# Attention and expert kernel: hand-written orders re-placed, one cast-load earlier, and the flag branches set ahead of the last stores

## The reference

```python
# layernorm of x as the graph's weights ("adj"), two layers of 8-head attention over ctx, elu after each
e = leaky_relu(attn_self[:, :, None] + attn_neigh[:, None, :], 0.2) + MASK_VAL * (1.0 - adj)[None, :, :]
out = elu(einsum('hnm,hmo->hno', softmax(e), feat) + b)
...
x = x + tanh(g_xattn[0]) * xattn(ctx_512, layernorm(x), W0, ..., b1)        # x: 4 x 256 x 256
# experts on xt = layernorm(x): 8 experts of 128 hidden columns, the best 2 of each token weighted
logits = tanh(xt @ Wg1.T) @ Wg2.T
h = silu(einsum('td,ehd->teh', xt, Wup) + bup)
down = einsum('teh,eoh->teo', h, Wdown) + bdown
x = x + tanh(g_ffn[0]) * einsum('te,teo->to', scores, down)
```

## Time and profile before

| | |
|---|---|
| runs | 87.66, 87.21, 87.19 us; median 87.21 |
| the profiled execution | 86.43 us, of which its span (first to last instruction) is 84.6 |
| granted TensorE clock | 0.997 |
| busy, share of the span | PE 90%, PE weight load 85%, DVE 79%, ACT 62%, POOL 47% |
| chain that ended last | PE 75%, DMA 6%, DVE 4%, issue 4%, ACT 4% |

### The profile page before, as it was taken

The page is one execution under the profiler, slowest core; times in us unless marked ns, Lnnn a source line. Parts: engine busy times, 40 slices in busy tenths (PEclk is TensorE's granted clock), DMA queues, the critical chain, the costliest instruction groups (busy, mean ns, idle before and its releaser), DMA issues.

```text
span 84.6 us, 1861 instructions
## 1 busy us (share of the span) xinstructions
PE 76.4 (90%) x571; PEld 72.2 (85%) x571; DVE 67.0 (79%) x217; ACT 52.5 (62%) x132; POOL 39.8 (47%) x85
## 2 busy tenths in 40 slices
PE   4999999998899999699999999999999999999400
PEld 4968887886899898599999999999999999999300
DVE  4896999898898583999997687599999574999500
ACT  0527999569957952777958668685786564662000
POOL 7990857978892807346504043000089877400000
PEclk9999999999999999999999999999999999999998
DMA  0999948207840183300000000019400079602130
GB/s 30 264 286 377 378 56 364 89 4 178 319 130 7 27 286 114 101 0 12 0 0 0 0 8 4 0 29 287 188 0 0 12 188 340 215 0 85 54 121 19
DMA packets 5498, 9.67 MB, mean 114 GB/s; under 512 B 1338, under 2 KB 4140, under 8 KB 5100
## 3 DMA queue, kind: packets, MB, share of 16 engines
q1 hardware_dynamic: 4860, 7.66, 27.6%
q0 software_dynamic: 464, 1.59, 6.3%
q10 hardware_dynamic: 160, 0.26, 1.6%
HBM read 7.90 MB, written 1.61 MB: 112 GB/s over the span
## 4 chain that ended last, share of the span: by engine, by line
PE 75%; DMA 6%; DVE 4%; issue 4%; ACT 4%; ACTq 1%; DVEq 0%
PE bank L872 9%; PE bank L874 9%; PE bank L873 9%; PE bank L827 8%; PE bank L828 8%; PE bank L832 7%; PE bank L953 6%; DMA ctx_sb<-in_ctx_t 6%; PE bank L942 3%; PE bank L978 2%; PE bank L768 2%; PE bank L847 2%; DVE hid_lo L1315 2%; PE bank L780 2%; DVE wdown_lo L1276 2%
## 5 line engine op out<-in xcount | busy, mean ns | idle before, releaser
L615 ACT CAST hid_hi<-hid 128x256 fp32r<-128x256 f32 x32 | 12.9, 404 | 10.6 <-DVE hid L1181 9.3
L872 PE MATMUL bank<-wdown_hi,hid_hi 128*128 128x256 f32 x64 | 18.2, 285 | 0.0
L827 PE MATMUL bank<-xt_hi,wup_hi 128*128 128x256 f32 x64 | 17.7, 299 | 0.4 <-ACT act_sb L607 0.4
L873 PE MATMUL bank<-wdown_lo,hid_hi 128*128 128x256 f32 x64 | 17.9, 279 | 0.0
L874 PE MATMUL bank<-wdown_hi,hid_lo 128*128 128x256 f32 x64 | 17.9, 279 | 0.0
L607 ACT ACTIVATE act_sb<-bank,small_sb 128x256 f32<-128x256 f32 x32 | 14.9, 468 | 4.1 <-PE bank L832 3.9
L828 PE MATMUL bank<-xt_hi,wup_lo 128*128 128x256 f32 x64 | 16.6, 281 | 0.0
L1188 DVE TENSOR_TENSOR hid_lo<-hid,hid_hi 128x256 fp32r<-128x256 f32 x32 | 13.4, 420 | 1.8 <-ACT hid_hi L615 1.6
L827 PEld LDWEIGHTS bank<-xt_hi,wup_hi 128*128 128x128 f32 x64 | 12.1, 189 | 0.8 <-ACT act_sb L607 0.6
L832 PE MATMUL bank<-xt_lo,wup_hi 128*128 128x256 f32 x64 | 12.7, 280 | 0.0
L828 PEld LDWEIGHTS bank<-xt_hi,wup_lo 128*128 128x128 f32 x64 | 12.1, 189 | 0.0
(11 more groups left out here) (160 smaller groups left out, 178.2 us busy)
## 6 DMA issues: line engine op xcount, KB each, us to landing
score_bc<-score_hbm SPq DMA_DIRECT2D x4, 512.0 KB, 4.7
x_sb<-in_x SPq DMA_DIRECT2D x4, 256.0 KB, 4.4
wup_sb<-in_wup SPq DMA_DIRECT2D x1, 1024.0 KB, 6.2
wdown_sb<-in_wdown SPq DMA_DIRECT2D x1, 1024.0 KB
wdown_hi<-in_wdown POOLq DMA_DIRECT2D x1, 1024.0 KB
out<-out_sb SPq DMA_DIRECT2D x3, 256.0 KB, 4.6
z_hbm<-elu_exp SPq DMA_DIRECT2D x2, 256.0 KB, 3.5
check_sb<-in_check_w SPq DMA_DIRECT2D x1, 320.0 KB
```

What stands on the lines that cost most here:

```text
L615: nc.scalar.copy(hid_hi[:, n % HID_SLOTS, :], hid[:, n % HID_BUFS, :]).then_inc(hid_hi_rdy, 1)
L827: nc.tensor.matmul(dst, wup_hi[:, c, cols], xt_hi[:, b, c, :], start=(c == 0), stop=False)
L872: nc.tensor.matmul(dst, hid_hi[:, n % HID_SLOTS, part], wdown_hi[:, e, :], start=False, stop=False, skip_group_check=True)
L873: nc.tensor.matmul(dst, hid_hi[:, n % HID_SLOTS, part], wdown_lo[:, e, :], start=False, stop=False, skip_group_check=True)
```

## The change

What it does:
- `on_general` takes a second function for the Else. DVE's `dve_finish` of the last batch and SP's last two stores are put into it (and into the general version), so that DVE and SP load the flag and branch before them.
- `wdown_high` goes ahead of `leaders(2)` in POOL's queue. POOL's three Wup quarters (now 0, 2, 1) follow each other behind `row_power(0)`; DVE's quarter is 3, after `elu1(3)`. The wait for xn is ahead of `fetch(2)` now, and `leaders(3)` between the two fetches.
- Calls of the front on PE, ACT and DVE are in another order, and the slot numbers of many steps are others.

```diff
-XT_LOW_AT = {5: 1, 13: 2, 18: 3}
+XT_LOW_AT = {6: 1, 14: 2, 17: 3}
-GATE_AT = {7: 1, 15: 2, 20: 3}
+GATE_AT = {10: 1, 16: 2, 19: 3}
...
-FINISH_AT = {24: 0, 30: 1, 38: 2}
+FINISH_AT = {18: 0, 29: 1, 35: 2}
-COUNT_AT = 37
+COUNT_AT = 35
...
-        def on_general(eng, body):
+        def on_general(eng, body, otherwise=None):
...
             with eng.Else():
-                eng.wait_ge(flag_rdy, 1)
+                if otherwise is None:
+                    eng.wait_ge(flag_rdy, 1)
+                else:
+                    otherwise()
...
+            def store_last(run):
                 for t in range(C):
                     sp.wait_ge(out_rdy, NT * (run + 1) - C + t + 1)
                     sp.dma_start(out[B - 1, t * P:(t + 1) * P, :], out_sb[:, NT - C + t, :]).then_inc(stored, 16)
...
             def general():
+                store_last(0)
...
-            on_general(sp, general)
+            on_general(sp, general, lambda: store_last(0))
...
             bdown_split()
+            wdown_high()
             leaders(2)
+            row_power(pool, 0, 0)
+            wup_part(0)
             wup_part(2)
-            row_power(pool, 0, 0)
-            wdown_high()
+            wup_part(1)
+            row_power(pool, 0, 1)
             pool.wait_ge(xn_rdy, C)
-            wup_part(0)
+            fetch(2)
             leaders(3)
-            wup_part(3)
-            row_power(pool, 0, 1)
-            fetch(2)
+            row_power(pool, 0, 2)
             fetch(3)
-            row_power(pool, 0, 2)
...
             minus0(3)
             exp0(3)
+            turned(1)
             wup_part(0)
             wup_part(1)
+            minus1(1)
+            exp1(1)
             wup_part(2)
...
             feat1(2, 0)
+            twice_part(1)
             feat1(2, 1)
-            twice_part(1)
...
             elu1(1)
             dve_norm(dve, 0)
-            wup_part(1)
+            rows_leader(3)
             z_low()
...
-            dve_finish(dve, run, B - 1)
...
-                                 27: [check_peak_max], 29: [check_peaks_all], 40: [check_flag]})
+                                 16: [lambda: wdown_part(3)], 20: [check_ctx], 23: [check_weights], 25: [check_small],
+                                 27: [check_peak_max], 29: [check_peaks_all], 39: [check_flag]})
...
-            on_general(dve, general)
+            on_general(dve, general, lambda: dve_finish(dve, 0, B - 1))
```

More of the change, by code:

```diff
@@ L52 @@
 SLOTS = STEPS + DOWN_LAG
-NORM_AT = {3: ((1, 0), (1, 1),), 10: ((2, 0), (2, 1),), 16: ((3, 0), (3, 1),)}
-XT_AT = {5: 1, 12: 2, 18: 3}
-XT_LOW_AT = {5: 1, 13: 2, 18: 3}
-GATE_AT = {7: 1, 15: 2, 20: 3}
[L57 to L61, removed]
-FINISH_AT = {24: 0, 30: 1, 38: 2}
+NORM_AT = {2: ((1, 0),), 3: ((1, 1),), 10: ((2, 0),), 12: ((2, 1),), 16: ((3, 0), (3, 1),)}
+XT_AT = {5: 1, 14: 2, 17: 3}
+XT_LOW_AT = {6: 1, 14: 2, 17: 3}
+GATE_AT = {10: 1, 16: 2, 19: 3}
+TANH_AT = {10: 1, 17: 2, 21: 3}
+SUM_AT = {10: 1, 16: 2, 21: 3}
+LOGITS_AT = {10: 1, 17: 2, 21: 3}
+DIFF_AT = {3: 0, 11: 1, 18: 2, 24: 3}
+SCORE_AT = {6: 0, 14: 1, 20: 2, 27: 3}
+FINISH_AT = {18: 0, 29: 1, 35: 2}
 CHECK_AT = 25
-COUNT_AT = 37
+COUNT_AT = 35
 FIRST_SPREAD = 2
@@ L391, in general @@
                 store(1)
-            on_general(sp, general)
+                store_last(1)
+            on_general(sp, general, lambda: store_last(0))
         def row_power(pool, run, b):
@@ L695, in _ @@
             minus0(1)
+            exp0(1)
             turned(0)
-            exp0(1)
             minus0(2)
             exp0(2)
-            gate_scale()
             minus1(0)
             exp1(0)
+            gate_scale()
             minus0(3)
             exp0(3)
+            turned(1)
             wup_part(0)
             wup_part(1)
+            minus1(1)
+            exp1(1)
             wup_part(2)
-            turned(1)
-            minus1(1)
+            source_copy(1)
             wup_part(3)
-            exp1(1)
-            source_copy(1)
+            z_high()
             minus1(2)
-            z_high()
+            act_xt(act, 0, 0)
             exp1(2)
-            act_xt(act, 0, 0)
             minus1(3)
@@ L1000, in _ @@
             feat0(3)
+            feat1(1, 0)
             turn(1)
-            feat1(1, 0)
             gather(0)
@@ L1322, in _ @@
             rows_top(2)
+            elu0(1)
             rows_leader(2)
-            elu0(1)
             source_copy()
@@ L1333, in _ @@
             dve_aggr(dve, 0, 0)
-            rows_leader(3)
             elu1(1)
             dve_norm(dve, 0)
-            wup_part(1)
+            rows_leader(3)
             z_low()
@@ L1345, in _ @@
             dve_logits(dve, 0, 0)
+            elu1(3)
+            wup_part(3)
             dve_route(dve, 0)
-            elu1(3)
             def check_ctx():
@@ L1385, in check_flag @@
                 nc.vector.tensor_copy(flag[:], flag_f[:]).then_inc(flag_rdy, 1)
[L1387 to L1390, removed]
-                                 27: [check_peak_max], 29: [check_peaks_all], 40: [check_flag]})
+            dve_experts(dve, 0, {4: [lambda: wdown_part(0)], 7: [lambda: wdown_part(1), lambda: gated(2)],
+                                 8: [lambda: dve_stats(dve, 0, 2), lambda: dve_aggr(dve, 0, 2)], 13: [lambda: wdown_part(2)],
+                                 14: [lambda: gated(3), lambda: dve_stats(dve, 0, 3)], 15: [lambda: dve_aggr(dve, 0, 3)],
+                                 16: [lambda: wdown_part(3)], 20: [check_ctx], 23: [check_weights], 25: [check_small],
+                                 27: [check_peak_max], 29: [check_peaks_all], 39: [check_flag]})
             def general():
+                dve_finish(dve, 0, B - 1)
                 nc.vector.memset(nmax[:], 0.0).then_inc(g_xa, 1)
@@ L1470, in general @@
                 dve_experts(dve, 1, {})
-            on_general(dve, general)
+                dve_finish(dve, 1, B - 1)
+            on_general(dve, general, lambda: dve_finish(dve, 0, B - 1))
 _OUT = ("out", (B, N, D))
```

## The result

The changed kernel takes **90.2 us** (median of 4 runs, 89.44 to 90.86), the one before 87.2 on the same chip: a ratio of 1.036 (1.021 to 1.051). Run once more on another occasion it gave 1.036 again (1.025 to 1.046; 89.03 against 86.83). I had forecast 86.4 with a range up to 87.9. The sign was wrong, and so was the range.

What follows compares the result with a forecast made beforehand. PE was taken as the bound, three quarters of the chain of waits. Span 84.6 - 1.5 (PE earlier) + 0.7 (tail) = 83.8, 0.8 less; 87.21 - 0.8 = 86.4 us, own range 85.7 to 86.9, overall 84.9 to 87.9.

Steps and rivals of the forecast that it cites:

- DVE's jump: Tail: DVE's way from compare to Else, 3.1 us, comes before the last outputs, which start 2.7 us late.
- Rival 3: Tail: DVE's jump costs nothing there, outputs keep their time; 85.0 us, or 83.6 with the landing; chance 0.12.
- The landing: Tail: the last stores find quiet queues and land in 2.1 us instead of 3.5, kept for the range.
- The tail's own sum: Behind PE's last matmul: late outputs and quicker landing together move the end from 84.6 to 85.3, costing 0.7 us.
- The front: Up to `gather(1)` on PE: if norm and shift alternate kindly, `z_low` comes sooner; 0.68 possible, 0.5 us taken.
- rival 1: Front: POOL takes the port between the two norms, `gather(1)` 0.3 later instead of 0.5 earlier; 87.2 us; chance 0.18.
- just in time: Front: POOL's rstd is done at 17.88, when DVE comes to the norm at 17.92.
- The port of the prediction: Front: DVE and POOL share a port, so one waits for the other's whole instruction.
- The middle: PE after `gather(1)`: earlier rows and a denser DVE give back 1.1 less 0.3, plus 0.2 us.
- What PE lost at 28.21: Middle: PE loses about 0.2 us before the transposes at 28.21, all counted as gained.
- the loss at the third pick: Middle: PE loses 1.1 us around the third pick at 34.18; all but 0.3 counted as given back.
- rival 2: Tail: DVE's jump eats more than PE's 1.5 gain; 88.1 us, or 87.9 if PE gains nothing; chance 0.20.

Runs made afterwards that it cites:

- experiment one: The kernel before with only the branches of DVE and SP moved ahead of the last outputs and stores; 89.16 us, 1.036 of before.
- experiment four: The changed kernel with DVE's two arms exchanged, so the usual finish directly follows the compare; 86.76 us, 0.990 of before.
- experiment five: experiment four with POOL waiting for both norms before its three Wup quarters; 84.69 us, 0.984 of before; again 85.48 us, 0.975.
- experiment twelve: experiment five without PE's flag load, branch and general version; 83.79 us, 0.978 of before.
- experiment eight: experiment one without PE's flag load, branch and general version; 88.17 us, 1.023 of before.
- experiment two: The changed kernel with its new orders but DVE's and SP's tail as before; 86.72 us, 1.008 of before.
- experiment six: experiment four with `row_power(pool, 0, 0)` moved ahead of `leaders(2)` on POOL; 84.74 us, 0.980 of before by the medians.
- experiment ten: experiment two with POOL waiting for both norms before its three Wup quarters; 86.23 us, 0.989 of before.
- experiment seven: experiment four with both the wait of experiment five and the move of experiment six; 84.82 us, 0.986 of before.

## Why the prediction was wrong, point by point

**DVE's jump: right.** I took 3.1 us from DVE's own row against ACT's 2.6 and PE's 4.1; it was 3.0 in three kernels. The compare came 0.6 before PE's last matmul (forecast: 0.4), and the outputs stood behind the jump and not behind PE, as written. Experiments one and four show the cause by adding it alone and by taking only the distance away. The traces show code coming in beside the jumps: PE's two `instruction` packets of 16 KB are there in experiment five and gone with its branch in experiment twelve. Counted in the program as built, DVE's jump passes over 353 of its 649 instructions; ACT's passes over 188 of 373 and takes 2.4 us. Rival 3, a jump that costs nothing here, is dead by DVE's 3.0.

**The landing: the step that failed in the tail.** "I take 2.1": measured 3.9. The tail's own sum corrected: 0.7, plus 1.8 for the landing, less 0.3 for outputs a little sooner than forecast, is the 2.2 measured. My reason was that the stores would find quiet queues once the jumps were done. But PE compares at 79.8 and needs 3.8 us, to 83.7, and the last store is issued at 83.2; the second code packet of PE, which follows even later, is under way until 85.9. By experiments eight and twelve PE's jump is what holds the stores up. I had counted DVE's jump ending and overlooked that PE's starts later and that its code still comes in beside the stores.

**The front: the step that failed on PE.** "If norm and shift alternate kindly ... I take 0.5." The kindness didn't come, and rival 1 did: the norms took 1.68 and `gather(1)` was 0.73 later, not 0.3 as that rival had it. The rival priced one Wup quarter between the norms, and had rstd at its old time. That rstd came at 17.98 is a second thing, and I had taken it as "just in time" without working it out: ahead of it stand the cast-load and the leaders' issues, behind a bias load that landed 1.3 us late. Experiment two tells which of the two matters: with rstd at 16.72 the transposes were no sooner. The quarter that runs between or beside the norms is the cause, and late rstd only puts the same loss elsewhere. Experiments five and six take the collision away in two ways; in their traces the norms are at 0.73 and PE's last matmul is 2.1 and 1.8 us sooner than in experiment four's. The times show less: experiment ten against experiment two, the clean pair, 1.9% or 1.6 us. The port of the prediction is a reading of these lengths; no run shows the port itself.

**The middle: missed as well.** I gave back 1.0; from `gather(1)` to its last matmul PE needed 57.6 us instead of 57.5, so nothing came of it. What PE lost at 28.21 is gone; of the loss at the third pick (1.1 in my sum, 1.27 counted from where a dense start would have been) 1.0 is still there, at 31.25 and 32.73, where ACT's `act_sb` on the bank before had ended at 31.19 and 32.67, just ahead of PE (that this holds PE up is read, not tried); DVE's wait before `gated(2)` is 0.96, not under 0.5. And a place that I had read as free became one: DVE's `hid` of the last batch waits for `score_bc` from DRAM, now 1.64 us at 71.99 instead of 1.13 at 71.30, and PE stands for `hid_hi` at 72.94, 0.5 us that were not there. In experiment five, with the front mended, PE needs 57.1 us for this stretch, 0.45 less than before. That its last matmul is where I had put it is in part luck: the front gave 0.9 where I had 0.5, and the middle 0.45 where I had 1.0.

**The rivals.** Rivals 1 and 2 came true together: the second ends at 87.9 if PE gains nothing. I had given them 0.18 and 0.20 and treated them as exclusive, and none of my outcomes had PE end later than before. 87.21 with 0.8 of PE and 2.2 of tail is 90.2, the time measured.

## What to carry to other kernels

DVE's path over an untaken block of some 350 instructions cost 3.0 us here: put the usual case in the arm that follows the compare, and let the far arm be the rare one. The jump over the far arm came all the same, 3.2 us behind the usual case in experiment four, so it wants something to hide behind, here the landing of the stores. A Wup quarter of POOL that was ready within DVE's pair of norms made the pair 1.68 us instead of 0.73, and two made it 2.68; with a DMA issue or a wait there instead (experiments six and five) it was 0.73, and that is what to try where a long operation of POOL stands beside a short chain of DVE. And when rivals concern different stretches, add them up, since they can all happen.

## What the runs showed of the hardware that I had not expected

- PE's jump, with its code in two packets of 16 KB, delays the stores: it costs the slower of the last ones 1.0 us on experiment one (2.8 to 1.8) and 0.7 on experiment five (3.1 to 2.4), though the code is 0.03 MB. The link is shown by leaving PE's branch out in two kernels. That it is the code which does it, and that the store's last packets stand behind a code packet on one of the DMA engines, are read from the changed kernel's trace, not tried by themselves. In experiment one the compare had ended at 82.5 and the last store was issued at 82.8; PE's second code packet was under way from 83.3 to 84.4, and the store still took 2.8.
- The stall of DVE's jump was 3.0 us with PE's branch and 3.0 without it in experiments one and eight, 3.2 and 2.8 in experiments five and twelve. It differs by engine over all the traces here: ACT 2.4 to 3.0 us, DVE 2.8 to 3.4, PE 3.5 to 4.2, over 188, some 350 and over 500 instructions, counted in the program as built. POOL and SP, with 38 and 27 to pass, take 0.2.
- POOL gets in between two consecutive operations of DVE of one call: a norm of 0.36 waited for one quarter in the changed kernel (1.68 for the pair) and for two in experiment two (2.68). Both lengths fit a norm that waits until POOL's operation is over; in both kernels the turns went against DVE.
- In the changed kernel PE's granted clock was 1.00 until 82 us, 0.78 in the next and 0.50 from 83 us on; PE had stood idle since 80.2. The mean of 0.971 is the tail alone and explains nothing of the loss.

Of the versions that leave nothing out none is faster by more than the scatter than experiment five, 84.69 and 85.48 us on two occasions, 0.984 and 0.975 of before; experiments six and seven stand beside it with 84.74 and 84.82.
